# Products with the edge aggregates: one fp32 pass over 65 rows, or two fp32r passes over 128 rows

## The chip, the cores and the metric

The kernel runs on one core of one Trainium2 chip. The metric is the device time of one execution in microseconds (us), lower is better. The engines are TensorE (PE; its weight loads are PEld), VectorE (DVE), ScalarE (ACT), GpSimd (POOL) and SyncE (SP), which here only issues DMAs. Each engine runs its own list of instructions in order and waits on semaphores for the others.

## The reference

Two layers of a graph network over 1024 nodes of 512 features, each with a layer norm, a graph part, an attention-like mixer and a feed-forward part. The change is in the graph part of the second layer:

```python
def _L1_gnn_ref(x, edge_index, edge_attr, u, batch, W1, b1, W2, b2):
    col = edge_index[1]
    summed = jax.ops.segment_sum(edge_attr, col, num_segments=x.shape[0])      # 33792 edges, 64 features
    count = jax.ops.segment_sum(jnp.ones((edge_attr.shape[0],)), col, num_segments=x.shape[0])
    agg = summed / jnp.maximum(count, 1.0)[:, None]                            # 1024 x 64
    h = jnp.concatenate([x, agg], axis=-1)                                     # 1024 x 576
    h = jax.nn.relu(h @ W1 + b1)                                               # 1024 x 1024
    return x + h @ W2 + b2
...
x = x + _L0_ffn_ref(layernorm(x))          # 16 experts, each token goes to one
xn = layernorm(x)
x = x + _L1_gnn_ref(xn, ...) + _L1_mix_ref(xn, ...)
```

So `h @ W1 + b1` is a product with the 512 features of `xn`, one with the 64 aggregates, and a bias.

## The kernel before

Large products keep fp32 accuracy with fp32r operands: each operand is split in a high part (a copy rounded to fp32r, made by ACT) and a low part (the rest, made by DVE), and `mm3` (lines 877 to 881) issues low x high, high x high and high x low, three matmuls of 512 columns. `L879`, `L880` and `L881` are these three, in every stage. Engines meet at numbered jobs: `finished(eng, job)` waits until PE has completed the job, `emptied(eng, job)` until its PSUM bank has been read out.

The work around the change comes in this order.

- The 16 experts. For expert e, PE turns the rows (`eT`), and computes `eY`. ACT copies the expert's weights to the high part (`L1474`), DVE subtracts the low part (`L1978`), DVE adds the bias (`L2022`), and ACT sends the result to DRAM (`send_y`, `L1321`). SP loads the experts' weights (`L763`) into a ring of six, each load after `ew_split` says that both halves of an earlier expert are split; behind them it loads the graph weights W1a and W2a into `xn` (`L716`).
- After the last expert ACT and DVE split W1a and W2a (`split_weight`, `L1344` and `L1619`), while POOL gathers the experts' results by row (`L846`). PE transposes the aggregates (`aggT`, `L1124`), DVE copies them out of PSUM (`L2027`) and sets a row of ones for the bias (`L2028`).
- DVE then adds the gathered rows (`routed`, `L2033`), takes the moments (`L1632`, `L1633`), normalises (`L1646`) two rows of tiles at a time, and PE turns them (`turn_rows`, `L887`); ACT and DVE split what was turned (`L1350`, `L1626`). The tiles t = 0 to 3 come first, 4 to 7 after PE has begun.
- The products H: for hh (half of the 1024 hidden columns), th (half of the tokens) and m (block of 128 columns) twelve matmuls by `mm3` and one call of `from_aggregates` (`L1129`), which multiplies the 64 rows of aggregates and the row of ones with W1's last 64 rows and the bias. These operands are fp32, in `w1e` and `aggT` with 65 rows. For the four H of hh = 0, th = 0 this call comes first, ahead of the transposes, for the other twelve it comes last. The products HW (with W2) follow each group of four H.

The trace shows each `from_aggregates` as two matmul instructions.

Of the kernel before, what the change touches and what calls it, by code (L numbers as in the profile page):

```python
# [310 lines left out]
def build(nc, a):  # L311
# [18 lines left out]
    with ExitStack() as ctx:  # L330
# [3 lines left out]
        def f32(ap):  # L334
            return ap[:].bitcast(F32)
# [38 lines left out]

        aggT = arena[0:EA + 1, 2 * AW:2 * AW + N]
        w1e = arena[0:EA + 1, 2 * AW + N:2 * AW + 2 * N]
        pring = arena[:, 3 * AW:4 * AW].rearrange("p (r i) -> p r i", r=4)
# [150 lines left out]
        res_ready = sem("res_ready")  # L528
        w1e_in = sem("w1e_in")
        l1_in = sem("l1_in")  # L530
        rowa_in = sem("rowa_in")
# [146 lines left out]
        def _(sp):  # L678
# [107 lines left out]
            for e in range(WRING, EXPERTS):  # L786
                load_expert(e)
            sp.wait_ge(res_ready, T)
            load_weight("W1a")
            load_weight("W2a")  # L790
            finished(sp, "eY", EXPERTS - 1)
            sp.dma_start(w1e[0:EA], a["L1_gnn_W1"][D:D + EA]).then_inc(w1e_in, 16)
            sp.dma_start(w1e[EA:EA + 1], a["L1_gnn_b1"].rearrange("(a n) -> a n", a=1)).then_inc(w1e_in, 16)
            sp.wait_ge(res_ready, 2 * T)
# [72 lines left out]
        def _(pe):  # L867
# [253 lines left out]
            for g in range(2):  # L1121
                o = open_bank("aggT", g)
                for j in range(4):
                    ins = pe.transpose(o[0:EA, chunk(j)], agg[:, 4 * g + j, :], ident)  # L1124
                close(ins)

            def from_aggregates(hh, th, m, start):
                ch = hh * C + m
                return pe.matmul(at("H", hh, th, m), w1e[:, ch * P:(ch + 1) * P], aggT[:, th * HALF:(th + 1) * HALF],  # L1129
                                 start=start, stop=not start)  # L1130

            pe.wait_ge(w1e_in, 32)
            pe.wait_ge(blk_ready, 1)
            for g in range(2):
# [28 lines left out]

            pe.wait_ge(blk_ready, 2)
            o = open_bank("csq")
# [162 lines left out]
        def _(act):  # L1328
# [152 lines left out]
            for e in range(EXPERTS):  # L1481
                if e >= 2:
                    expert_high(e, 0)
                finished(act, "eT", e)
                act.activation(xbT[e % 2][:, 0], at("eT", e)[:, 0:C * CAPR].rearrange("p (c s) -> p c s", c=C), ACT.Copy).then_inc(xb_hi, 1)
                if e >= 2:
                    expert_high(e, 1)
                    send_y(act, e - 2)
            send_y(act, EXPERTS - 2)
            send_y(act, EXPERTS - 1)  # L1490
            split_weight("W1a")
            split_weight("W2a")
# [111 lines left out]
        def _(dve):  # L1604
# [404 lines left out]
            for e in range(EXPERTS + 1):  # L2009
# [6 lines left out]
                if e > 0:  # L2016
# [3 lines left out]
                    if y >= Y_RING:  # L2020
                        dve.wait_ge(y_out[y % Y_RING], 16 * (y // Y_RING))
                    dve.tensor_tensor(ey[y % Y_RING], at("eY", y)[0:CAPR, :], eb[y % 4], ALU.add).then_inc(evicted[bank_of[("eY", y)]], 1)  # L2022
            split_weight("W1a")
            split_weight("W2a")
            for g in range(2):
                finished(dve, "aggT", g)
                dve.tensor_copy(aggT[0:EA, g * HALF:(g + 1) * HALF], at("aggT", g)[0:EA, :]).then_inc(evicted[bank_of[("aggT", g)]], 1)  # L2027
            dve.memset(aggT[EA:EA + 1, :], 1.0).then_inc(blk_ready, 1)  # L2028
            dve.wait_ge(res_ready, T)
# [21 lines left out]
            for t in range(2, TH):  # L2051
                lo(("xT", 2, t))
            for t in range(TH, T):
                if t > TH:
                    routed(t)
                routed_moments(t)
# [261 lines left out]
```

## Time and profile before

| what | value |
|---|---|
| three runs | 906.35, 908.46, 911.83 us; median 908.46 us |
| the profiled execution | 909.68 us, span of its instructions 907.9 us |
| PE busy | 803.0 us, 88% of the span |
| PE weight loads | 575.9 us |
| DVE busy | 630.3 us, 69% |
| ACT busy | 372.4 us, 41% |
| POOL busy | 102.4 us, 11% |
| mean granted TensorE clock | 0.951 of full |

Busy times overlap between the engines. Matmuls are pipelined, and their ends are modelled: the distance from one start to the next tells what a matmul costs, not its own duration. "Idle before" is how long an engine had nothing to do, and the name behind it who released it.

### The profile page before, as it was taken

The page shows a single profiled execution, that of the slowest core. Times are in us where ns is not written, and L with a number is a line of the kernel's source. Part 1 is how long each engine was busy: PE and PEld are TensorE (multiplying, and loading weights), DVE is VectorE, ACT ScalarE, POOL GpSimd, SP SyncE. Part 2 cuts the span into 40 slices and gives each one's busy share as a digit, 9 for nine tenths or more (in the row PEclk, how much of TensorE's full clock was granted, in tenths as well). Part 3 has the DMA queues.
Part 4 walks back from the last instruction along what each step waited for, and adds up shares of the span by engine and source line. Part 5 has one row for each costly group of instructions (what it writes and reads, how often), then busy time and mean ns, then how long its engine had stood idle before and what let it go on. Part 6 is the DMA issues. An engine that isn't in the chain of part 4 may idle for free. (4 is left out here: it accounts for less than half of the span.)

```text
span 907.9 us, 11554 instructions
## 1 busy us (share of the span) xinstructions
PE 803.0 (88%) x4058; PEld 575.9 (63%) x4058; DVE 630.3 (69%) x1207; ACT 372.4 (41%) x557; POOL 102.4 (11%) x76
## 2 busy tenths in 40 slices
PE   5999999999999960895899998998797999999788
PEld 3777888888778840563587777555463445446564
DVE  7667776776749557598853232778867888884976
ACT  2342343332313240475112117756315887884150
POOL 3000000000000005012280004443100000000010
PEclk9989999999999995898599999999898999999999
DMA  5571312210302414996311102000001000000002
GB/s 173 150 250 49 107 56 71 71 36 8 117 1 92 147 65 138 286 373 233 97 66 47 47 22 72 1 1 1 2 2 48 1 1 1 1 0 1 6 1 93
DMA packets 48152, 66.63 MB, mean 73 GB/s; under 512 B 4268, under 2 KB 22460, under 8 KB 48095
## 3 DMA queue, kind: packets, MB, share of 16 engines
q1 hardware_dynamic: 43903, 56.22, 19.4%
q0 software_dynamic: 2384, 6.92, 2.3%
q10 hardware_dynamic: 1808, 2.75, 0.8%
q8 instruction: 33, 0.54, 0.2%
q14 instruction: 24, 0.20, 0.1%
HBM read 56.38 MB, written 9.50 MB: 73 GB/s over the span
## 5 line engine op out<-in xcount | busy, mean ns | idle before, releaser
L879 PE MATMUL bank<-xT,slot 128*128 128x512 f32 (+1 forms) x248 | 105.9, 427 | 5.7 <-DVE xT L1626 5.7
L880 PE MATMUL bank<-xT,slot 128*128 128x512 f32 (+1 forms) x248 | 98.5, 397 | 0.0
L881 PE MATMUL bank<-xT,slot 128*128 128x512 f32 (+1 forms) x248 | 98.2, 396 | 0.0
L1350 ACT ACTIVATE slot<-bank 128x512 fp32r<-128x512 f32 (+3 forms) x60 | 34.2, 586 | 144.3 <-PE bank L1129 56.3
L879 PE MATMUL bank<-slot 128*128 128x512 f32 (+1 forms) x212 | 85.2, 402 | 4.1 <-issue 1.8
L2131 DVE TENSOR_REDUCE key<-bank 128x2 f32<-128x1024 f32 x64 | 75.2, 1218 | 14.5 <-PE bank L1189 14.5
L879 PE MATMUL bank<-slot,xT 128*128 128x512 f32 (+1 forms) x192 | 79.2, 412 | 3.7 <-DVE arena L2194 2.8
L881 PE MATMUL bank<-slot 128*128 128x512 f32 (+1 forms) x212 | 81.9, 386 | 0.0
L880 PE MATMUL bank<-slot 128*128 128x512 f32 (+1 forms) x212 | 81.8, 386 | 0.0
L881 PE MATMUL bank<-slot,xT 128*128 128x512 f32 (+1 forms) x192 | 77.0, 401 | 0.0
L1563 ACT ACTIVATE arena<-bank 128x1024 f32<-128x1024 f32 x64 | 65.7, 1027 | 27.7 <-PE bank L1255 27.6
L880 PE MATMUL bank<-slot,xT 128*128 128x512 f32 (+1 forms) x192 | 77.0, 401 | 0.0
L879 PEld LDWEIGHTS bank<-xT,slot 128*128 128x128 f32 (+1 forms) x248 | 47.1, 190 | 21.5 <-issue 12.4
L880 PEld LDWEIGHTS bank<-xT,slot 128*128 128x128 f32 (+1 forms) x248 | 47.2, 190 | 11.0 <-issue 2.2
L881 PEld LDWEIGHTS bank<-xT,slot 128*128 128x128 f32 (+1 forms) x248 | 47.1, 190 | 11.2
L859 POOL TENSOR_TENSOR split_sq<-xn,split_sq 128x1024 fp32r<-128x1024 f32 x16 | 39.2, 2451 | 125.7 <-ACT split_sq L1526 125.7
L2174 DVE TENSOR_TENSOR slot<-arena,slot 128x1024 fp32r<-128x1024 f32 x43 | 52.4, 1218 | 0.2 <-ACT slot L1553 0.2
L879 PEld LDWEIGHTS bank<-slot 128*128 128x128 f32 x212 | 40.5, 191 | 15.7 <-issue 6.1
L833 POOL DMA_INDIRECT expert_rows<-xn,idx x8 | 10.2, 1276 | 322.3 <-DVE idx L1970 320.2
L879 PEld LDWEIGHTS bank<-slot,xT 128*128 128x128 f32 (+1 forms) x192 | 34.7, 181 | 18.1 <-issue 6.1
L881 PEld LDWEIGHTS bank<-slot 128*128 128x128 f32 x212 | 40.5, 191 | 8.2
L880 PEld LDWEIGHTS bank<-slot 128*128 128x128 f32 x212 | 40.6, 192 | 7.9 <-issue 0.7
(323 smaller groups left out, 1647.5 us busy)
## 6 DMA issues: line engine op xcount, KB each, us to landing
arena<-in_ewT SPq DMA_DIRECT2D x16, 1024.0 KB, 11.5
arena<-in_edge_attr SPq DMA_DIRECT2D x16, 512.0 KB, 4.0
wraw<-in_qkvT SPq DMA_DIRECT2D x3, 1024.0 KB, 5.2
expert_rows<-rows SPq DMA_DIRECT2D x1, 2560.0 KB, 14.0
wraw<-in_L_ffn_expert_b POOLq DMA_DIRECT2D x16, 160.0 KB, 5.8
expert_results<-wraw ACTq DMA_DIRECT2D x16, 160.0 KB, 5.7
xn<-in_x SPq DMA_DIRECT2D x4, 512.0 KB, 6.3
wraw<-in_L_mix_w_qkv SPq DMA_DIRECT2D x2, 1024.0 KB, 7.8
```

The costliest lines, as they stand in the source:

```text
L833: pool.indirect_dma_start(xbuf, bass.IndirectOffsetOnAxis(ap=idx[:, 0, t:t + 1], axis=0), xn[:, t, :], None).then_inc(rows_sent, 16)
L859: pool.tensor_tensor(split_sq[:, i % 4, 1], raw_sq[:, i % 4], f32(split_sq[:, i % 4, 0]), ALU.subtract).then_inc(sq_lo, 1)
L879: pe.matmul(out, L[1], R[0], start=start, stop=False, **kw)
L880: pe.matmul(out, L[0], R[0], start=False, stop=False, **kw)
L881: return pe.matmul(out, L[0], R[1], start=False, stop=stop, **kw)
L1350: act.activation(h, src, kw.pop("func", ACT.Copy), **kw).then_inc(hi_done, 1)
L1563: act.activation(pexp[:, n % 3], bank[:, b:b + 2, :], ACT.Exp).then_inc(evicted[b], 1)
L2131: dve.tensor_reduce(mxh[:, c % 2, jh, :, it:it + 1], bank[:, b:b + 2, :], AX, ALU.max).then_inc(evicted[b], 1)
L2174: dve.tensor_tensor(psplit(n % 3, 1), pexp[:, n % 3], f32(psplit(n % 3, 0)), ALU.subtract).then_inc(p_lo, 1)
```

## The change

`from_aggregates` issues two fp32r matmuls over 128 rows in place of one fp32 matmul over 65. The operands are stacked:

- `agg_rows[:, 0]` holds the high part of the aggregates in rows 0 to 63 and the low part in rows 64 to 127; `agg_w[:, 0]` holds the high part of the weights twice. Their product is high x high plus high x low.
- `agg_rows[:, 1]` holds the high part again in rows 0 to 63 and ones below; `agg_w[:, 1]` holds the low part of the weights, and below it zeros, with the bias' high part in row 64 and its low part in row 96.

To have the aggregates in all 128 rows, ACT writes `agg` twice side by side (`agg_twice`) behind its last work on expert 15, and PE transposes that. SP loads the 64 rows of W1 twice and the bias twice, after both halves of expert 11 are split (`ew_split` 24), ahead of W1a and W2a; before it loaded them once, after the last expert. ACT makes the high parts of these weights and of the bias (3 instructions) and of the transposed aggregates (4), ahead of splitting W1a. DVE fills (2 memsets), makes the low parts (2 and 2), splits W1a, and goes to the gathered rows; its part of splitting W2a moves behind the transposes' low parts of t = 0 to 3. The copies `L2027` and the memset `L2028` go.

```diff
--- before.py
+++ after.py
@@ -372,8 +372,11 @@
         ering = arena[:, AW:AW + WRING * C * D].rearrange("p (w c d) -> p w c d", w=WRING, c=C)
         gath = arena[:, AW:2 * AW].rearrange("p (t d) -> p t d", t=T)
 
-        aggT = arena[0:EA + 1, 2 * AW:2 * AW + N]
-        w1e = arena[0:EA + 1, 2 * AW + N:2 * AW + 2 * N]
+        agg_rows = nc.alloc_sbuf_tensor_at("agg_rows", [P, 2, N], F32R, offset=arena_at + 4 * 2 * AW)
+        agg_w = nc.alloc_sbuf_tensor_at("agg_weights", [P, 2, N], F32R, offset=arena_at + 4 * (2 * AW + 2 * N))
+        agg_twice = arena[:, 3 * AW:3 * AW + 2 * T * EA].rearrange("p (t v e) -> p t v e", t=T, v=2)
+        w1e = arena[:, 3 * AW + N:3 * AW + 2 * N]
+        b1e = arena[:, 3 * AW + 2 * N:3 * AW + 3 * N]
         pring = arena[:, 3 * AW:4 * AW].rearrange("p (r i) -> p r i", r=4)
         VW = T * HEADS * (HD + 1)
         vone = nc.alloc_sbuf_tensor_at("vone", [P, 2, T, HEADS, HD + 1], F32R, offset=arena_at + 4 * AW)
...
@@ -785,12 +793,14 @@
                 load_rows(group)
             for e in range(WRING, EXPERTS):
                 load_expert(e)
+            sp.wait_ge(ew_split, 2 * (EXPERTS - WRING + 2))
+            for v in range(2):
+                sp.dma_start(w1e[EA * v:EA * (v + 1)], a["L1_gnn_W1"][D:D + EA]).then_inc(w1e_in, 16)
+            for row in (EA, EA + 32):
+                sp.dma_start(b1e[row:row + 1], a["L1_gnn_b1"].rearrange("(a n) -> a n", a=1)).then_inc(w1e_in, 16)
             sp.wait_ge(res_ready, T)
             load_weight("W1a")
             load_weight("W2a")
-            finished(sp, "eY", EXPERTS - 1)
-            sp.dma_start(w1e[0:EA], a["L1_gnn_W1"][D:D + EA]).then_inc(w1e_in, 16)
-            sp.dma_start(w1e[EA:EA + 1], a["L1_gnn_b1"].rearrange("(a n) -> a n", a=1)).then_inc(w1e_in, 16)
             sp.wait_ge(res_ready, 2 * T)
             for name in ("W1b", "W2b", "Lq", "Lk", "Lv", "Lo"):
                 load_weight(name)
@@ -1120,17 +1130,20 @@
 
             for g in range(2):
                 o = open_bank("aggT", g)
+                pe.wait_ge(agg_copied, 2)
                 for j in range(4):
-                    ins = pe.transpose(o[0:EA, chunk(j)], agg[:, 4 * g + j, :], ident)
+                    ins = pe.transpose(o[:, chunk(j)], agg_twice[:, 4 * g + j].rearrange("p v e -> p (v e)"), ident)
                 close(ins)
 
             def from_aggregates(hh, th, m, start):
                 ch = hh * C + m
-                return pe.matmul(at("H", hh, th, m), w1e[:, ch * P:(ch + 1) * P], aggT[:, th * HALF:(th + 1) * HALF],
-                                 start=start, stop=not start)
-
-            pe.wait_ge(w1e_in, 32)
-            pe.wait_ge(blk_ready, 1)
+                o, w = at("H", hh, th, m), slice(th * HALF, (th + 1) * HALF)
+                pe.matmul(o, agg_w[:, 0, chunk(ch)], agg_rows[:, 0, w], start=start, stop=False)
+                return pe.matmul(o, agg_w[:, 1, chunk(ch)], agg_rows[:, 1, w], start=False, stop=not start)
+
+            pe.wait_ge(agg_high, 4)
+            pe.wait_ge(agg_w_high, 2)
+            pe.wait_ge(agg_ready, 1)
             for g in range(2):
                 emptied(pe, "aggT", g)
             for m in range(C):
@@ -1161,7 +1174,7 @@
                                 waits=lambda k: t == 0 and emptied(pe, "H", hh, th, k))
 
 
-            pe.wait_ge(blk_ready, 2)
+            pe.wait_ge(blk_ready, 1)
             o = open_bank("csq")
             for c in range(PAIRS):
                 ins = pe.matmul(o[:, c:c + 1], csquare[:, chunk(c)], ones[:, 0:1], start=True, stop=True)
@@ -1486,8 +1499,21 @@
                 if e >= 2:
                     expert_high(e, 1)
                     send_y(act, e - 2)
+            for v in range(2):
+                act.activation(agg_twice[:, :, v, :], agg[:, :, :], ACT.Copy).then_inc(agg_copied, 1)
             send_y(act, EXPERTS - 2)
             send_y(act, EXPERTS - 1)
+            act.wait_ge(w1e_in, 64)
+            act.activation(agg_w[:, 0, :], w1e, ACT.Copy).then_inc(agg_w_high, 1)
+            act.wait_ge(agg_filled, 1)
+            for row in (EA, EA + 32):
+                ins = act.activation(agg_w[row:row + 1, 1, :], b1e[row:row + 1], ACT.Copy)
+            ins.then_inc(agg_w_high, 1)
+            for g in range(2):
+                finished(act, "aggT", g)
+                w = slice(g * HALF, (g + 1) * HALF)
+                act.activation(agg_rows[:, 0, w], at("aggT", g), ACT.Copy).then_inc(agg_high, 1)
+                act.activation(agg_rows[0:EA, 1, w], at("aggT", g)[0:EA], ACT.Copy).then_inc(agg_high, 1)
             split_weight("W1a")
             split_weight("W2a")
             for g in range(2):
@@ -2020,12 +2046,18 @@
                     if y >= Y_RING:
                         dve.wait_ge(y_out[y % Y_RING], 16 * (y // Y_RING))
                     dve.tensor_tensor(ey[y % Y_RING], at("eY", y)[0:CAPR, :], eb[y % 4], ALU.add).then_inc(evicted[bank_of[("eY", y)]], 1)
+            dve.memset(f32(agg_w)[EA:P, 1, :], 0.0).then_inc(agg_filled, 1)
+            dve.memset(f32(agg_rows)[EA:P, 1, :], 1.0)
+            dve.wait_ge(agg_w_high, 2)
+            dve.tensor_tensor(agg_w[0:EA, 1, :], w1e[0:EA], f32(agg_w)[0:EA, 0, :], ALU.subtract)
+            low = slice(EA + 32, EA + 33)
+            dve.tensor_tensor(agg_w[low, 1, :], b1e[low], f32(agg_w)[low, 1, :], ALU.subtract).then_inc(agg_ready, 1)
+            for g in range(2):
+                dve.wait_ge(agg_high, 2 * g + 1)
+                w, lows = slice(g * HALF, (g + 1) * HALF), slice(EA, P)
+                dve.tensor_tensor(agg_rows[lows, 0, w], at("aggT", g)[lows], f32(agg_rows)[lows, 0, w], ALU.subtract).then_inc(
+                    evicted[bank_of[("aggT", g)]], 1)
             split_weight("W1a")
-            split_weight("W2a")
-            for g in range(2):
-                finished(dve, "aggT", g)
-                dve.tensor_copy(aggT[0:EA, g * HALF:(g + 1) * HALF], at("aggT", g)[0:EA, :]).then_inc(evicted[bank_of[("aggT", g)]], 1)
-            dve.memset(aggT[EA:EA + 1, :], 1.0).then_inc(blk_ready, 1)
             dve.wait_ge(res_ready, T)
             dve.wait_ge(rows_sent, 16 * T)
             def routed(t):
@@ -2050,6 +2082,7 @@
             routed(TH)
             for t in range(2, TH):
                 lo(("xT", 2, t))
+            split_weight("W2a")
             for t in range(TH, T):
                 if t > TH:
                     routed(t)
```

What stands in a row on PE around each of the twelve later calls, in the products H of hh = 0, th = 1 (`xT` is the turned xn, `slot` the weights, `arena` the aggregates and their weights). Before:

```order
L880 MATMUL bank<-xT,slot 128x512
L881 MATMUL bank<-xT,slot 128x512
L1129 MATMUL bank<-arena 128x512
L879 MATMUL bank<-xT,slot 128x512
L880 MATMUL bank<-xT,slot 128x512
```

And in the changed kernel, where mm3's lines are 889 to 891:

```order
L891 MATMUL bank<-xT,slot 128x512
L1141 MATMUL bank<-agg_rows,agg_weights 128x512
L1142 MATMUL bank<-agg_rows,agg_weights 128x512
L889 MATMUL bank<-xT,slot 128x512
L890 MATMUL bank<-xT,slot 128x512
```

One matmul became two, and nothing else moved there.

On DVE behind the last expert (`L2022` and `L2048` add its bias; `slot<-xn` is a weight's low part). Before:

```order
L2022 TENSOR_TENSOR wraw<-bank,wraw 80x512 x2
L1619 TENSOR_TENSOR slot<-xn,slot 128x2048 x2
L2027 COPY arena<-bank 64x512 x2
L2028 MEMSET arena 1x1024
L2033 SCALAR_TENSOR_TENSOR arena<-arena,cols 128x512 x2
L1632 BN_STATS cols<-arena 128x6
```

And now:

```order
L2048 TENSOR_TENSOR wraw<-bank,wraw 80x512 x2
L2049 MEMSET agg_weights 64x1024
L2050 MEMSET agg_rows 64x1024
L2052 TENSOR_TENSOR agg_weights<-arena,agg_weights 64x1024
L2054 TENSOR_TENSOR agg_weights<-arena,agg_weights 1x1024
L2058 TENSOR_TENSOR agg_rows<-bank,agg_rows 64x512 x2
L1645 TENSOR_TENSOR slot<-xn,slot 128x2048
L2065 SCALAR_TENSOR_TENSOR arena<-arena,cols 128x512 x2
L1658 BN_STATS cols<-arena 128x6
```

Six instructions stand where three stood, and one of the two weight splits is gone from here. It comes back further down, behind the low parts of the turned tiles (`xT<-bank,xT`). Before and now:

```order
L2033 SCALAR_TENSOR_TENSOR arena<-arena,cols 128x512
L1626 TENSOR_TENSOR xT<-bank,xT 128x4x128 x2
L1632 BN_STATS cols<-arena 128x6
```

```order
L2065 SCALAR_TENSOR_TENSOR arena<-arena,cols 128x512
L1652 TENSOR_TENSOR xT<-bank,xT 128x4x128 x2
L1645 TENSOR_TENSOR slot<-xn,slot 128x2048
L1658 BN_STATS cols<-arena 128x6
```

On ACT behind the last two results sent (`expert_results`), before and now:

```order
L1321 DMA expert_results<-wraw 80x512 [waits evicted7]
L1344 ACTIVATE slot<-xn 128x2048 [waits mm_done,w_in2]
L1344 ACTIVATE slot<-xn 128x2048 [waits mm_done,w_in3]
L1355 ACT_TABLE_LOAD
```

```order
L1334 DMA expert_results<-wraw 80x512 [waits evicted7]
L1507 ACTIVATE agg_weights<-arena 128x1024 [waits w1e_in]
L1510 ACTIVATE agg_weights<-arena 1x1024 [waits agg_rows_filled]
L1510 ACTIVATE agg_weights<-arena 1x1024
L1515 ACTIVATE agg_rows<-bank 128x512 [waits mm_done]
L1516 ACTIVATE agg_rows<-bank 64x512
L1515 ACTIVATE agg_rows<-bank 128x512 [waits mm_done]
L1516 ACTIVATE agg_rows<-bank 64x512
L1357 ACTIVATE slot<-xn 128x2048 [waits mm_done,w_in2]
L1357 ACTIVATE slot<-xn 128x2048 [waits mm_done,w_in3]
L1368 ACT_TABLE_LOAD
```

Seven instructions stand ahead of the high part of W1a, for which DVE waits.

## Rows read from the trace of the kernel before

**Rows 1.** Waits of PE from 445 to 560 us: engine, line, releaser, total, times, longest.

```profile
PE bank L879 <- DVE xT L1626: 1.5, 1, 1.5
```

**Rows 2.** Stretches: length, busy time by engine, granted clock (PEclk), DMA share, GB/s.

```profile
434.00:436.00 2.00, 2.00 (x4) 0.86 (x3) 1.93 (x6) 0.20 (x1) 1.70 (x2) 0.50 0.68 182
...
450.00:451.00 1.00, 1.00 (x5) 0.81 (x4) 0.97 (x2) 0.00 (x0) 0.00 (x0) 0.79 0.07 16
...
452.00:460.00 8.00, 8.00 (x42) 6.73 (x41) 4.20 (x9) 2.51 (x5) 5.66 (x5) 1.00 0.70 259
```

**Rows 3.** PE in order of time, 462 to 478 us: start, duration, instruction.

```profile
462.67 0.39 PE L879 MATMUL bank<-slot 128*128 128x512 f32 x1
...
471.29 0.39 PE L881 MATMUL bank<-slot 128*128 128x512 f32 x1
...
474.24 1.02 PE L1129 MATMUL bank<-arena 65*128 65x512 f32 x2
...
475.33 0.40 PE L880 MATMUL bank<-xT,slot 128*128 128x512 f32 x1
...
477.84 1.02 PE L1129 MATMUL bank<-arena 65*128 65x512 f32 x2
```

**Rows 4.** Line 1129 alone: durations, first and last start.

```profile
L1129 PE MATMUL bank<-arena x32: 590/592/1191, 431.2 to 536.1; 65*128 65x512 f32 x32
```

**Rows 5.** All engines in order of time, 422 to 446 us.

```profile
422.25 3.71 ACT L1344 ACTIVATE slot<-xn 128x2048 fp32r<-128x2048 f32 x2 [5.26 <-PE bank L1124]
424.19 4.49 DVE L1619 TENSOR_TENSOR slot<-xn,slot 128x2048 fp32r<-128x2048 f32 x2 [2.39 <-ACT slot L1344]
...
430.14 0.91 DVE L2028 MEMSET arena<- 1x1024 f32 x1 [0.27 <-issue]
431.09 1.59 DVE L2033 SCALAR_TENSOR_TENSOR arena<-arena,cols 128x512 f32<-128x512 f32 x2
...
431.16 7.16 PE L1129 MATMUL bank<-arena 65*128 65x512 f32 x8 [9.20 <-DVE arena L2028]
...
436.08 1.00 DVE L1646 TENSOR_SCALAR xn<-arena,cols 128x512 f32<-128x512 f32 x2
...
438.12 1.91 PE L887 MATMUL bank<-kst,xn 128*128 128x128 f32 x8
...
440.56 0.20 ACT L1355 ACTIVATE cols<-cols 128x2 f32<-128x2 f32 x1
...
441.49 1.00 DVE L1646 TENSOR_SCALAR xn<-arena,cols 128x512 f32<-128x512 f32 x2
...
443.25 0.60 ACT L1350 ACTIVATE xT<-bank 128x512 fp32r<-128x512 f32 x1 [2.49 <-PE bank L887]
...
445.57 0.76 PE L879 MATMUL bank<-xT,slot 128*128 128x512 f32 x1 [1.50 <-DVE xT L1626]
```

**Rows 6.** Groups by line and shape, ACT and DVE, 395 to 425 us.

```profile
L1474 ACT ACTIVATE slot<-arena 128x1024 fp32r<-128x1024 f32 x14 | 14.8, 1055 | 6.5 <-PE bank L881 6.5
L1978 DVE TENSOR_TENSOR slot<-arena,slot 128x1024 fp32r<-128x1024 f32 x15 | 18.1, 1207 | 0.0
```

**Rows 7.** In order of time, 452 to 460 us: tiles 4 to 7, and four ACT copies.

```profile
452.12 1.91 DVE L1646 TENSOR_SCALAR xn<-arena,cols 128x512 f32<-128x512 f32 x4
...
458.86 1.91 PE L887 MATMUL bank<-kst,xn 128*128 128x128 f32 x16
...
459.55 2.07 ACT L1350 ACTIVATE xT<-bank 128x512 fp32r<-128x512 f32 x4
```

**Rows 8.** SP's DMA issues, 395 to 401 us.

```profile
396.35 3.63 SPq L763 DMA_DIRECT2D arena<-in_ewT  x2
400.03 3.25 SPq L716 DMA_DIRECT2D xn<-in_L_gnn_W  x1
```

**Rows 9.** DMA issues from 395 us on: size, median us from issue to landing.

```profile
arena<-in_ewT SPq DMA_DIRECT2D x2, 1024.0 KB, 14.5
xn<-in_L_gnn_W SPq DMA_DIRECT2D x2, 1024.0 KB, 17.7
```

More of the change, by code:

```diff
@@ L529, in build @@
         w1e_in = sem("w1e_in")
+        agg_copied = sem("agg_copied")
+        agg_high = sem("agg_rows_high")
+        agg_w_high = sem("agg_weights_high")
+        agg_ready = sem("agg_rows_ready")
+        agg_filled = sem("agg_rows_filled")
         l1_in = sem("l1_in")
```

## The prediction

> **What bounds the kernel now.** I read the waits first, then the order of time around line 1129. From 445 to 560 us, where all products H and HW lie, PE waits once, 1.5 us at the very start [rows 1]: that stretch is bound by PE, and an instruction that PE loses there shortens it by its full slot. Ahead of it, from 422 to 445 us, the order of time shows the opposite: PE idles 9.20 us until DVE's memset, runs eight pieces of line 1129, then turns tiles as DVE delivers them [rows 5]. There the chain is ACT's high part of W1a, DVE's low parts, copies and memset, the gathered rows, the normalised tiles, their transposes. So the change is priced twice: slots of PE behind 445.6 us, lateness of DVE's chain before.
>
> **PE's slots.** The durations of pipelined matmuls overlap, so I count starts. From 462.67 to 471.29 us there are 38 steps of one 128x512 product: 8.62 / 38 = 0.227 us each [rows 3]. One block H goes from 474.24 to 477.84 us, 3.60 us; its twelve products take 12 x 0.227 = 2.72, which leaves 0.88 us for the call of line 1129 [rows 3]. The 32 pieces are 16 calls [rows 4], 12 of them at the end of a block, in the PE-bound stretch. Two fp32r products cost 2 x 0.227 = 0.45 us, if operands in 128 rows stream as all other operands do. Saved: 0.88 - 0.45 = 0.43 us a call, 12 x 0.43 = 5.2 us. The matmuls behind them read nothing new, and what waits for H (ACT's and DVE's reads) only comes sooner.
>
> The four early calls take 7.16 us, at a granted clock of 0.50 [rows 2, 5], the 1.2 GHz level. As eight products at that level they take 8 x 2 x 0.21 = 3.4 us. They count only as far as they hold up the first transposes: tile 0 is normalised half of 1.00 us behind 436.08, at 436.6, while PE comes free and starts turning at 438.12 [rows 5]. Those 1.5 us are what the early calls cost now.
>
> **The chain on ACT and DVE ahead of the gathered rows.** ACT is free for this at 422.25 [rows 5]. Three copies of 1024 columns: 1.06 us each, overlapping to some 0.96 [rows 6], so 2.9 us. (No row has a copy on one partition. I take the 128-partition price, the dearest; the 0.20 us of a two-column ACTIVATE [rows 5] bounds it below, 1.5 us less for both.) Four copies out of PSUM: 2.07 us for four tiles [rows 7]. The high part of W1a follows at 422.25 + 2.9 + 2.0 = 427.2 and takes 1.9 (half of 3.71, rows 5), until 429.0. DVE's two memsets (0.91 each by the 1x1024 one, which lie in its idle time of 2.39 us, rows 5) and four subtractions (2 x 1.21 [rows 6], 2 x 0.7) fit between: weights from 425.2 to 427.6, aggregates to 429.05. Then W1a's low part, 2.25 (half of 4.49), until 431.3. The gathered rows start at 431.3 where they started at 431.09 [rows 5]: 0.2 us later. Gone are W2a's low part, both copies and the memset; the ACT work put ahead of W1a takes nearly all of that back. PE's early products run from 429.1 to 432.5, out of everybody's way.
>
> Then the rest of the chain moves by 0.2: tile 0 is ready at 436.85 instead of 436.6, but PE is free, so it is turned at once. DVE's low parts of tiles 0 and 1, which waited for ACT, follow its moments without the gap, and the normalisation of tiles 2 and 3, at 441.49 now, comes at about 440.85. From it to PE's first product of H the distance stays 445.57 - 441.49 = 4.1 us [rows 5]. H starts at 444.9: **0.65 us gained**. Bounds: if the copies on one partition are as short as they may be, 1.5 more at most, less what DVE then lacks (its own subtractions end at 429.05 less the same), together 2.1; if no copy overlaps the next and each handover costs 0.2 us, 1.4 less, -0.7.
>
> **What is moved.** W2a's low part, 2.25 us, now stands ahead of the moments of tiles 4 to 7. Their normalisation starts at 452.12 now and PE turns them at 458.86 [rows 7], 6.7 us later. In the change it starts at 452.1 + 2.25 - 0.65 = 453.7, and PE comes at 458.2: covered, with 4.5 us to spare; without that cover each us costs one. POOL's additions and the loads of W1b and W2b wait for the same tiles, and move by 1.6 us; POOL needs its first result only where HW is read, behind 461 us.
>
> **DMA.** SP issues expert 15's load at 399.6 and W1a's at 400.03 [rows 8]; they land 14.5 and 17.7 us later, one behind the other [rows 9]. Now SP waits for two experts more, 2 x 3.26 = 6.5 us (the distance of two loads in rows 8: 3.63 - 0.37), until 406.1, and issues 0.5 MB in four DMAs before W1a. Expert 15's load lands near 414, so the queues never run dry; the stacked weights land by 416, W1a by 419.5 and W2a by 422.3. ACT wants them at 422.25, 427.2 and 429: hidden. The aggregates' two copies stand on ACT while PE still has experts 14 and 15: hidden.
>
> **Sum.** 5.2 + 0.65 = 5.85 us off the profiled execution's 909.68 gives 903.8. The runs before have the median 908.46, which gives 902.6; I predict between, **903.3 us**. By its unknowns this case goes from 901 to 906.
>
> **The granted clock.** H begins at 445.57 at the low level, which still holds in 434 to 436; from 450 to 451 it is 0.79, and 1.00 after [rows 2]: the clock comes up at about 450.4. So 4.8 us of H run at half speed, which costs 2.4 us. The early calls, 7.16 us of unbroken PE work, did not lift it [rows 2, 5]. The Trainium skill ("TensorE: Matmul & The Clock Gate", "What's actually happening") has it that the throttled state is the default and sustained activity releases it. Here it did not for the fp32 products. By the page's rule nothing sets the fp32r ones apart, by the trace fp32r products did lift it at 450.4.
>
> **Rivals.**
> - *The clock comes up for H sooner*, since the early calls are now of the kind that lifts it. Gain up to 2.4 us more: 901.0. Against it: between 432.5 and 436.9 PE is idle, longer than now, and transposes alone did not lift it either.
> - *It comes up later*, or drops once more, by as much: 905.7. For it: less PE work ahead of H; against it: the stretch from 445 on is as dense as before.
> - *ACT's chain is the new wait.* Seven copies with no overlap take 3 x 1.06 + 4 x 0.60 = 5.6 for 4.9, with handovers 6.3. Each us shifts W1a's low part, the gathered rows and H by one. The gain is 5.2 - 0.7 = 4.5: 904.6.
> - *The fp32r pair brings nothing*: if the pair still took 0.88, the start alone stays, 908.4. Against it stand all steps of 0.227 in rows 3; operands of lines 879 to 881 have the same form.
> - *SP's queue turns the sign.* W1a's issue occupies SP for 3.25 us with full queues [rows 8]. If each of the four new DMAs does so too, W1a is issued at 406.1 + 13 = 419.1 and, landing 17.7 us later, is there at 436.8 for 427.2. DVE's chain is late by 9.6, less the 5.85: 3.8 us slower, 912.8. It decides from 427.2 + 5.85 = 433 on. Against it: two of the four carry 4 KB, and by then nothing but expert 15's load is queued.
>
> **How the numbers follow.** Forecast 0.55; clock sooner 0.09, later 0.09; ACT's chain 0.14; no saving 0.07; SP's queue 0.06. Single runs before lie 906.35 to 911.83 apart, so a median moves by 1.5 or so without any cause. From 900.0 to 907.0 us the range leaves out the last two cases, half of the clock's early one at its far end, and little of the rest. A measurement tells 0.5% from nothing, 4.5 us. The forecast's 5.85 lies 1.3 above that, so it counts 0.75 as faster; the sooner clock fully; of the later clock and ACT's chain four in ten. Faster 0.60, within 0.5% 0.34, slower 0.06.
>
> **What would show it.** Twelve blocks H of 3.18 us where they were 3.60; the early products over by about 432.5; the gathered rows from 431.3; the first transposes right behind the first normalised tile; H at 444.9; PE without a wait at tiles 4 to 7; W1a landed before 427. I am wrong if a block stays at 3.6, if the gathered rows begin later than 433, or if PE waits for tile 4.

## The result and the profile after

The changed kernel took 902.64 us, the median of 20 runs (898.71 to 907.72), against 907.07 for the kernel before on the same chips (20 runs, 905.13 to 911.83). The ratio over all of these runs is 0.9944, 95% interval 0.9929 to 0.9960: 5.1 us faster, between 3.6 and 6.4. (The two medians alone lie 4.4 us apart.) The forecast was 903.3 us, a gain of 5.85 us. The profiled execution took 903.49 us, its span 901.7. Of the executions behind this document, one of the run `both` (947.57 us) and two of the kernel before that were taken beside it (1301.79 and 1928.99 us) were in a slower state, and the ratios and the medians given leave them out.

The first part of the profile's page, busy time by engine (before: 803.0, 630.3 and 372.4 us for PE, DVE and ACT):

```profile
PE 795.4 (88%) x4058; PEld 576.2 (64%) x4058; DVE 634.7 (70%) x1210; ACT 378.3 (42%) x566; POOL 103.0 (11%) x76
```

PE has as many instructions as before (a call was two pieces and is two products) and is busy 7.6 us less; DVE and ACT are busy 4 and 6 us more. What shortened is PE's list, and the chain through the other two had to bear more work. In order of time on PE, one block H of the changed kernel, against [rows 3]:

```profile
471.25 0.39 PE L1141 MATMUL bank<-agg_rows,agg_weights 128*128 128x512 f32 x1
471.48 0.39 PE L1142 MATMUL bank<-agg_rows,agg_weights 128*128 128x512 f32 x1
471.71 0.39 PE L889 MATMUL bank<-xT,slot 128*128 128x512 f32 x1
...
474.43 0.39 PE L1141 MATMUL bank<-agg_rows,agg_weights 128*128 128x512 f32 x1
```

The two products start 0.23 us apart like any others, and the block takes 3.18 us where it took 3.60. The same stretch as in [rows 5], all engines in order of time, from the last expert's bias add on:

```profile
418.67 0.69 DVE L2048 TENSOR_TENSOR wraw<-bank,wraw 80x512 f32<-80x512 f32 x1 [1.34 <-PE bank L891]
...
419.74 1.06 ACT L1507 ACTIVATE agg_weights<-arena 128x1024 fp32r<-128x1024 f32 x1 [3.50 <-DVE wraw L2048]
...
420.82 2.12 ACT L1510 ACTIVATE agg_weights<-arena 1x1024 fp32r<-1x1024 f32 x2
...
422.97 1.22 DVE L2052 TENSOR_TENSOR agg_weights<-arena,agg_weights 64x1024 fp32r<-64x1024 f32 x1 [1.36 <-ACT agg_weights L1510]
...
425.02 3.71 ACT L1357 ACTIVATE slot<-xn 128x2048 fp32r<-128x2048 f32 x2
...
426.96 2.29 DVE L1645 TENSOR_TENSOR slot<-xn,slot 128x2048 fp32r<-128x2048 f32 x1 [0.21 <-ACT slot L1357]
427.00 0.76 PE L1141 MATMUL bank<-agg_rows,agg_weights 128*128 128x512 f32 x1 [7.50 <-DVE agg_rows L2058]
...
429.18 1.41 DVE L2065 SCALAR_TENSOR_TENSOR arena<-arena,cols 128x512 f32<-128x512 f32 x2
...
434.58 1.97 PE L897 MATMUL bank<-kst,xn 128*128 128x128 f32 x8 [3.82 <-DVE xn L1672]
...
442.44 0.76 PE L889 MATMUL bank<-xT,slot 128*128 128x512 f32 x1 [1.50 <-DVE xT L1652]
```

The bias add ends at 419.36 here. In the kernel before it ended at 421.81:

```profile
421.12 0.69 DVE L2022 TENSOR_TENSOR wraw<-bank,wraw 80x512 f32<-80x512 f32 x1 [1.33 <-PE bank L881]
```

These 2.45 us can't be laid to the change: in eight profiles of kernels that are the same up to there (the change's among them), the add ended anywhere between 418.5 and 424.0 us. So distances are what to compare. PE's early products are over 3.8 us before the first transposes, which now follow the first normalised tile. Up to W1a's low part ACT sets the pace: DVE waits 1.36 us for the copies of the bias and 0.21 for W1a's high part. From there on it is DVE's.

The executions, cut at three events: the end of DVE's bias add of expert 15, the start of PE's first product of H, and the start of the second product behind the last call of the aggregates. (It is the second because the first one's row, 0.80 us long, begins inside the call where the call is fp32.) The last cut, before and after:

```profile
536.76 0.40 PE L880 MATMUL bank<-slot 128*128 128x512 f32 x1
```

```profile
528.60 0.39 PE L890 MATMUL bank<-slot 128*128 128x512 f32 x1
```

In us:

| stretch | before | after | difference |
|---|---|---|---|
| start to the last expert's bias add | 421.81 | 419.36 | -2.45 |
| from there to the first product of H | 23.76 | 23.08 | -0.68 |
| from there to the second product behind the last call | 91.19 | 86.16 | -5.03 |
| the rest of the span | 371.14 | 373.10 | +1.96 |

The two stretches of the change, in the middle, give -5.71 us. The first holds only the loads moved ahead and ACT's two copies of `agg`, the last holds no edit, and both differ by no more than profiles of kernels do that are the same there. The last one differs by the clock; these are its stretches, first of before, then of after, to be read at PEclk (third number from the end):

```profile
536.00:908.00 372.00, 333.48 (x1442) 204.90 (x1440) 273.04 (x376) 203.44 (x281) 44.51 (x20) 0.97 0.05 16
```

```profile
528.00:902.00 374.00, 335.97 (x1443) 207.07 (x1441) 273.01 (x376) 203.41 (x281) 44.51 (x20) 0.96 0.05 15
```

DVE, ACT and POOL do the same work to 0.03 us, and only PE's busy time follows the granted clock. In thirteen profiles of kernels that are the same from there on, the last stretch took 368.7 to 373.4 us. A forecast of 5 us is therefore read from the distances, and the medians of many runs only confirm it.

### The profile page after: what moved, and what is told of

It is laid out like the page before. It is cut to its first block and busy times, and to the rows that moved or that the text cites. A ratio compares the mean times of both kernels' runs of the same rounds, so it can differ in the third digit from the quotient of the medians.

```text
span 901.7 us, 11571 instructions
## 1 busy us (share of the span) xinstructions
PE 795.4 (88%) x4058; PEld 576.2 (64%) x4058; DVE 634.7 (70%) x1210; ACT 378.3 (42%) x566; POOL 103.0 (11%) x76
## 5 line engine op out<-in xcount | busy, mean ns | idle before, releaser
L889 PE MATMUL bank<-slot 128*128 128x512 f32 (+1 forms) x212 | 83.3, 393 | 4.0 <-issue 1.8
L891 PE MATMUL bank<-slot 128*128 128x512 f32 (+1 forms) x212 | 81.6, 385 | 0.0
L890 PE MATMUL bank<-slot 128*128 128x512 f32 (+1 forms) x212 | 81.5, 384 | 0.0
```

What stands on the lines that cost most here:

```text
L889: pe.matmul(out, L[1], R[0], start=start, stop=False, **kw)
L890: pe.matmul(out, L[0], R[0], start=False, stop=False, **kw)
L891: return pe.matmul(out, L[0], R[1], start=False, stop=stop, **kw)
```

## Experiments

All times of the runs are medians, and each ratio is to the kernel before as timed beside that run; "distance" is that from the last bias add's end to H's first product (23.76 before, 23.08 after), from one profile of each.

| run | median us (runs) | ratio to before, interval | rows after add | distance |
|---|---|---|---|---|
| the change | 902.64 (20) | 0.9944, 0.9929 to 0.9960 | 9.82 | 23.08 |
| late_fp32 | 908.39 (12) | 1.0010, 0.9994 to 1.0027 | 9.82 | 23.10 |
| early_fp32 | 904.11 (10) | 0.9958, 0.9938 to 0.9977 | 9.82 | 23.09 |
| w2a_back | 901.98 (6) | 0.9940, 0.9919 to 0.9960 | 12.02 | 25.30 |
| late_load | 904.19 (12) | 0.9967, 0.9952 to 0.9982 | 13.71 | 26.98 |
| before_w2a_later | 905.40 (12) | 0.9982, 0.9967 to 0.9997 | 8.02 | 21.86 |
| clock_kept | 897.27 (6) | 0.9895, 0.9876 to 0.9914 | 9.82 | 22.39 |
| weights_early | 900.96 (7) | 0.9946, 0.9918 to 0.9974 | 8.13 | 22.67 |
| both | 899.05 (5) | 0.9906, 0.9881 to 0.9932 | 8.13 | 21.92 |

"Rows after add" is the start of DVE's first gathered row behind that add (9.28 before).

### The twelve later calls as one fp32 matmul

```diff
+                if not start:
+                    return pe.matmul(o, f32(agg_w)[:, 0, chunk(ch)], f32(agg_rows)[:, 0, w], start=False, stop=True)
```

> The changed kernel, with the twelve later calls as one fp32 matmul over the same 128 rows (the second product, with the weights' low part and the bias, is left out there; the four early calls stay two fp32r products). My theory: the gain lies in these slots. A block H takes 3.60 us again (12 x 0.227 + 0.88) where it takes 3.17 now, the twelve cost 12 x 0.43 = 5.2 us, and the time is about 907.8 against 902.6; the distance from the last expert's bias add to the first product of H stays 23.1 us. Rival: the gain came from the chain ahead of H and from a slower start of the kernel before; then the time stays within 1.5 us of 902.6.

Measured: 908.39 us, 5.75 above the change, all of the gain gone, with the distance unmoved. PE in order of time:

```profile
474.45 1.02 PE L1142 MATMUL bank<-agg_rows,agg_weights 128*128 128x512 f32 x2
474.91 0.80 PE L889 MATMUL bank<-xT,slot 128*128 128x512 f32 x1
...
478.08 1.02 PE L1142 MATMUL bank<-agg_rows,agg_weights 128*128 128x512 f32 x2
```

A block takes 3.63 us, 0.45 more than with two fp32r products, and with 128 rows nearly what it took with 65 (3.60). Twelve times 0.45 is 5.4. The stretch from H's start to the second product behind the last call took 90.45 us in this profile, 4.3 more than in the change and not 5.4: the clock came up 2.9 us behind H's start here and 5.3 there, and 2.4 us less at half speed are worth 1.2. The theory of the slots stands, the rival falls.

### The four early calls as one fp32 matmul

```diff
+                if start:
+                    return pe.matmul(o, f32(agg_w)[:, 0, chunk(ch)], f32(agg_rows)[:, 0, w], start=True, stop=False)
```

> The changed kernel, with the four early calls as one fp32 matmul each over 128 rows (the second product is left out in those four; the twelve later calls are as changed). They take 7.2 us again in place of 3.4, but lie ahead of the first transposes, which come 7.5 us behind their start. Theory: the fp32r form lifted the clock (the changed kernel has it at 1.00 from about 431 to 434 us, the kernel before stayed at 0.50 through 7.16 us of fp32 products). Then this run stays at 0.50 from 427 to the middle of H, and its time is within 1 us of the changed kernel's, since the lifted clock fell again before H. Rival: the form has nothing to do with it and only the place in time decides; then the clock rises during the early fp32 products too.

Measured: the distance, 23.09, is the change's, as expected of work off the path. The time, 904.11, is 1.5 us above the change's, where under 1 was expected, but the two intervals overlap widely. The theory of the clock was wrong. Three stretches of 2 us, PEclk third from the end:

```profile
428.00:430.00 2.00, 2.00 (x3) 0.74 (x3) 2.00 (x3) 1.75 (x2) 1.83 (x1) 0.50 0.52 137
430.00:432.00 2.00, 2.00 (x5) 0.61 (x3) 1.90 (x5) 0.00 (x0) 1.56 (x2) 0.91 0.57 143
432.00:434.00 2.00, 0.21 (x1) 0.00 (x0) 1.93 (x6) 0.20 (x1) 1.47 (x2) 1.00 0.74 172
```

The clock rose during fp32 products too, at about 430.4 us, and the rest of them ran fast. The form is not the cause; the last three experiments come back to it.

### DVE's low part of W2a back in its old place

```diff
             split_weight("W1a")
+            split_weight("W2a")
...
                 lo(("xT", 2, t))
-            split_weight("W2a")
```

> The changed kernel, with DVE's low part of W2a back in its old place, right behind that of W1a and ahead of the gathered rows. Theory: DVE is the chain there, so the gathered rows and the first product of H come 2.3 us later (25.4 us behind the last expert's bias add in place of 23.1), and the time is 904.9. Rival: the gathers' landing holds the rows up, so that 2.3 us of DVE work ahead of them cost under 1 us: 902.6 to 903.5.

DVE and PE in order of time:

```profile
435.30 1.41 DVE L2066 SCALAR_TENSOR_TENSOR arena<-arena,cols 128x512 f32<-128x512 f32 x2
...
448.58 0.77 PE L889 MATMUL bank<-xT,slot 128*128 128x512 f32 x1 [1.50 <-DVE xT L1652]
```

The add ends at 423.28 here: the rows start 12.02 us behind it, 2.20 later than in the change, and H 25.30, 2.22 later. In the chain the theory holds to 0.1 us. The median does not show it: 901.98 of six runs, where 904.9 was expected. Its interval, 0.9919 to 0.9960, leaves out 0.9968, which is the change's ratio and the 2.2 us, by less than the change's own interval is wide. The rest of the span was 369.2 us in this profile against 373.1 in the change, and 369.0 in clock_kept, where H is early; whether a later H helps it or the six runs fell well is open.

### The weights' last rows loaded behind the experts

```diff
-            sp.wait_ge(ew_split, 2 * (EXPERTS - WRING + 2))
-            for v in range(2):
-                sp.dma_start(w1e[EA * v:EA * (v + 1)], a["L1_gnn_W1"][D:D + EA]).then_inc(w1e_in, 16)
-            for row in (EA, EA + 32):
-                sp.dma_start(b1e[row:row + 1], a["L1_gnn_b1"].rearrange("(a n) -> a n", a=1)).then_inc(w1e_in, 16)
             sp.wait_ge(res_ready, T)
             load_weight("W1a")
             load_weight("W2a")
+            finished(sp, "eY", EXPERTS - 1)
+            for v in range(2):
+                sp.dma_start(w1e[EA * v:EA * (v + 1)], a["L1_gnn_W1"][D:D + EA]).then_inc(w1e_in, 16)
+            for row in (EA, EA + 32):
+                sp.dma_start(b1e[row:row + 1], a["L1_gnn_b1"].rearrange("(a n) -> a n", a=1)).then_inc(w1e_in, 16)
```

> The changed kernel, with the four DMAs of W1's last rows and the bias issued behind the last expert, as the kernel before does with its two. Theory: ACT's first copy waits for them: four issues of 0.5 us and a landing of 2 to 3 us put it at about 4.5 us behind PE's last product of the experts instead of 1.1, so the gathered rows and H come 3 to 3.5 us later, and the time is 905.6 to 906.1. Rival: the load is hidden in both places, as it was in the kernel before; then the time stays at 902.6 and the early load brings nothing.

```profile
422.25 1.06 ACT L1507 ACTIVATE agg_weights<-arena 128x1024 fp32r<-128x1024 f32 x1 [8.03 <-DMA arena<-in_L_gnn_b]
```

The add ends at 417.97; ACT begins 4.28 us behind it, released by the bias' DMA, where it began 0.38 behind it in the change. The distance grew by 3.90 us, where 3 to 3.5 were expected, all of that wait. The median grew by 1.55, to 904.19 where 905.6 to 906.1 was expected, and 0.9967 stands against the change's 0.9944 with intervals that overlap: in the chain the theory holds, and the time alone shows neither it nor its rival. The early load is needed by this form of the products: the kernel before needed its operands 9.3 us behind the add and could load late.

### The kernel before, with W2a's low part later

The same move as the change's, in the kernel before: `split_weight("W2a")` taken from behind that of W1a and put behind `lo(("xT", 2, t))` of tiles 2 and 3.

> The kernel before (one fp32 matmul a call), with the one change that DVE's low part of W2a stands behind the low parts of tiles 2 and 3, where the change put it. Theory: the move is what shortens the chain, and the change spends nearly all of it on ACT's seven copies. Then here the gathered rows start 7.0 to 7.8 us behind the last expert's bias add in place of 9.28, PE's early fp32 calls (7.16 us) then hold up the first transposes by about 1 us, and H starts 21.8 to 22.2 us behind that add in place of 23.76: 1.8 us off the kernel before, about 0.998 of its time. Blocks H stay at 3.60 us. Rival: the chain gains nothing from the move (the gathers' landing is what the rows wait for); then the distance stays at 23.8.

```profile
429.55 0.75 DVE L2032 SCALAR_TENSOR_TENSOR arena<-arena,cols 128x512 f32<-128x512 f32 x1 [0.97 <-DMA arena<-expert_results,idx]
430.91 0.75 DVE L2032 SCALAR_TENSOR_TENSOR arena<-arena,cols 128x512 f32<-128x512 f32 x1 [0.61 <-DMA arena<-expert_results,idx]
...
443.39 0.76 PE L879 MATMUL bank<-xT,slot 128*128 128x512 f32 x1 [1.50 <-DVE xT L1626]
```

The move alone shortens the distance by 1.90 us, to 21.86, and the kernel by 0.18% (0.03 to 0.33). That is more than the 0.68 us of the whole change. By this difference, the change's seven ACT copies and six DVE instructions spend 1.2 us of what the move brings. DVE now waits for the gathers' landing, 0.97 and 0.61 us: the chain has reached its next limit, and the rows start 8.02 us behind the add where 7.0 to 7.8 was expected. PE's early calls held the transposes up by nothing that shows: these start 0.60 us behind the normalisation, as in the change, where 1 us more was expected.

### Products nobody reads, ahead of H

```diff
+FILL = (11, 8, 6)
...
-            for t in range(TH):
+            def keep_busy(bank_at, count):
+                for _ in range(count):
+                    pe.matmul(bank[:, bank_at, :], agg_w[:, 0, chunk(0)], agg_rows[:, 0, 0:HALF], start=True, stop=True)
+
+            open_bank("xT", 2, 3)
+            keep_busy(bank_of[("xT", 2, 3)], FILL[0])
+            for t in range(2):
+                turn_rows(2, t)
+            keep_busy(bank_of[("xT", 2, 3)], FILL[1])
+            for t in range(2, TH):
                 turn_rows(2, t)
+            emptied(pe, "xT", 2, 0)
+            keep_busy(bank_of[("xT", 2, 0)], FILL[2])
```

> The changed kernel, with products nobody reads in PE's idle time ahead of H: 11 behind the early calls, 8 behind the transposes of tiles 0 and 1, 6 behind those of tiles 2 and 3, each 128x512 fp32r into a bank that is written over later or has been read. Theory: H starts at the low clock level because PE idles ahead of it, and that costs 2.4 to 2.6 us. Then the granted clock is 1.00 at H's start, the stretch from H's start to its last call takes 83.1 us in place of 85.7, the transposes are shorter by 0.5 us twice, and the time is 899.5 to 900. Rival: the filling products hold the transposes up by as much as the clock gives back (they run at half speed until the clock rises); then the time stays within 1 us of 902.6. A second rival: the clock falls in spite of them, and H takes 85.7 us.

PE in order of time, and the stretch at H's start:

```profile
429.57 2.68 PE L1155 MATMUL bank<-agg_rows,agg_weights 128*128 128x512 f32 x11
433.69 1.11 PE L898 MATMUL bank<-kst,xn 128*128 128x128 f32 x8 [1.44 <-DVE xn L1684]
434.56 2.09 PE L1155 MATMUL bank<-agg_rows,agg_weights 128*128 128x512 f32 x8
438.09 1.12 PE L898 MATMUL bank<-kst,xn 128*128 128x128 f32 x8 [1.44 <-DVE xn L1684]
438.96 1.62 PE L1155 MATMUL bank<-agg_rows,agg_weights 128*128 128x512 f32 x6
440.85 0.47 PE L890 MATMUL bank<-xT,slot 128*128 128x512 f32 x1 [0.27 <-DVE xT L1664]
```

```profile
440.00:442.00 2.00, 1.73 (x8) 1.17 (x7) 2.00 (x3) 0.00 (x0) 0.00 (x0) 1.00 0.04 8
```

The transposes find the clock at 1.00 and take 1.11 instead of 1.97 us. The distance fell by 0.69 us, and from H's start to its last call it took 83.29 us instead of 85.71, 2.42 less, which is the forecast's 2.4. That is 3.1 us by the distances. The median fell by 5.4, to 897.27 (by the ratios, 4.4), below the 899.5 to 900 expected; in the profile the rest of the span was 4.1 us shorter too, which these products do not touch, so more than 3.1 is not shown to be theirs. Both rivals fall. It has the lowest median here, and its interval and the change's do not overlap.

### The weights' work out of the chain, and both together

```diff
+            pool.wait_ge(ew_split, 2 * EXPERTS)
+            pool.memset(f32(agg_w)[EA:P, 1, :], 0.0).then_inc(agg_filled, 1)
+            pool.memset(f32(agg_rows)[EA:P, 1, :], 1.0).then_inc(agg_filled, 1)
...
             send_y(act, EXPERTS - 2)
+            act.wait_ge(w1e_in, 64)
+            act.wait_ge(ew_split, 2 * EXPERTS)
+            act.activation(agg_w[:, 0, :], w1e, ACT.Copy).then_inc(agg_w_high, 1)
             send_y(act, EXPERTS - 1)
...
+            split_weight("W1a")
```

The last line stands twice, on ACT and on DVE, each time ahead of the aggregates' parts.

> The changed kernel, with the work for the aggregates' weights taken out of the chain: GpSimd does both memsets as soon as expert 15's weights are split, ACT makes the weights' high part ahead of sending the last expert's result, and W1a's split stands ahead of the transposed aggregates' four copies on ACT and their low parts on DVE. Theory: DVE's gathered rows start 8.0 us behind the last expert's bias add in place of 9.82, the gathers' landing takes back up to 0.9 us of it, and H starts 21.5 to 22.1 us behind the add in place of 23.1: the time is 901.0 to 901.6. Rival: the gathers' landing is the next wait in full (the first is issued 3.9 us behind the add and lands 3.6 later, the others follow 1.3 to 2 us apart), and under 0.5 us is left: 902.1 and more.

```profile
427.79 0.75 DVE L2069 SCALAR_TENSOR_TENSOR arena<-arena,cols 128x512 f32<-128x512 f32 x1
...
429.71 0.75 DVE L2069 SCALAR_TENSOR_TENSOR arena<-arena,cols 128x512 f32<-128x512 f32 x1 [1.17 <-DMA arena<-expert_results,idx]
```

The first row starts 8.13 us behind the add, 1.69 earlier; the second then waits 1.17 us for its gather, and of the 1.69 only 0.41 reaches H (22.67). The rival was right in the chain: under 0.5 us is left. The median, 900.96, is what the theory expected and not the rival's 902.1, but its interval does not tell it apart from the change's.

> The two versions before this one together: the weights' work out of the chain, and products nobody reads in PE's idle time. If the two gains are independent, H starts 21 us behind the last expert's bias add and takes 83.1 us to its last call: 898 to 898.6. If the filling products now stand in the way of the transposes, which come sooner, the time is that of the better one of the two alone.

Measured: distance 21.92 and 83.29 us to the last call, 105.21 in sum against 105.68 in clock_kept and 108.79 in the change. In the distances the two gains add up (0.41 and 0.69 on their own, 1.16 together); H does not start at the 21 us expected because weights_early brings only 0.41. The median is 899.05, above the 898 to 898.6 expected and above clock_kept's 897.27, and its interval overlaps clock_kept's: the half microsecond is not to be seen in the time.

### What made the clock rise

The early calls stand above as fp32r over 128 rows (the change) and as fp32 over 128 rows (early_fp32). The three kernels here, each with one profile, have them as fp32 over 65 rows, as fp32r over 65, and as fp32r over 128 in the same place and number as the second.

> The changed kernel, with the four early calls as one fp32 matmul each over 65 of the 128 rows (the rest of their product is left out). It differs from early_fp32 in the rows alone. Seen so far: the clock came up at 430 to 433 us during or right behind early calls over 128 rows, of fp32 (early_fp32) and of fp32r, and stayed at 0.50 through 7.16 us of fp32 over 65 rows (the kernel before, and before_w2a_later). Theory: the count of rows is what matters; then the clock stays at 0.50 from the early calls to the middle of H. Rival: the place in time decides; then it rises at 430 to 434 here as well. The time is told by a single run and decides nothing: 899 to 907.

> The changed kernel, with each of the four early calls as four fp32r products over 65 of the rows in place of two over 128 (what they compute is not the reference's part; two of the four are repeats): 16 x 0.43 = 6.8 us of unbroken work at the low level. Theory of the rows: the clock stays at 0.50 through them, as under fp32 over 65 rows. Rival, the form: fp32r lifts it, so it rises to 1.00 within them.

> The same sixteen early fp32r products over all 128 rows (repeats, not the reference's part): the counterpart of early_fp32r_65. Both theories: the clock rises within them, so that the rest of them runs at 0.23 us each and the sixteen take under 6.8 us. If it does not rise here, rows and form are both out, and the place in time decides.

Line of the early calls in each, fp32 over 65 rows, then fp32r over 65, then fp32r over 128:

```profile
L1142 PE MATMUL bank<-agg_rows,agg_weights x8: 1061/1061/1192, 428.2 to 434.3; 65*128 65x512 f32 x8
```

```profile
L1143 PE MATMUL bank<-agg_rows,agg_weights x16: 628/628/766, 426.8 to 433.4; 65*128 65x512 f32 x16
```

```profile
L1143 PE MATMUL bank<-agg_rows,agg_weights x16: 387/628/763, 431.7 to 437.3; 128*128 128x512 f32 x16
```

And a stretch of 2 us near the end of these products in the second, and in the third:

```profile
432.00:434.00 2.00, 2.00 (x5) 1.00 (x4) 1.92 (x6) 0.20 (x1) 1.57 (x2) 0.50 0.74 174
```

```profile
436.00:438.00 2.00, 1.71 (x7) 1.02 (x5) 1.90 (x6) 0.20 (x1) 1.39 (x3) 0.94 0.66 215
```

Over 65 rows the clock stayed at 0.50 through 7.2 us of unbroken products, in fp32 and in fp32r, and came up only after H had begun; over 128 rows it rose within them, in both forms. The theory of the rows stands on these two pairs of profiles, one in each form, and on the kernel before and before_w2a_later (65 rows, 7.2 us, no rise). It does not say all: late_fp32 is the change itself up to H, its early products took the same 3.75 us, and the clock did not rise there before H. The times of these three, 901.97, 903.81 and 905.75 us, are of single runs and tell nothing.

## Why the prediction was right

- **PE's slots** (forecast 5.2 us less). 5.03 measured from H's start to behind its last call, block by block 3.60 to 3.18. Confirmed by late_fp32, which gives it all back. The missing 0.2 is the clock: it came up 5.3 us behind H's start instead of 4.8, at about 447.7.
- **The chain** (forecast 0.65 us less). 0.68 measured. The mechanism was right: ACT's copies eat what the moved split gives, and before_w2a_later shows both sides, 1.90 less by the move and, by difference, 1.22 spent. That the number is so near is luck: two errors of a third of a us cancel. The gathered rows start 0.54 us later against the add, not 0.2. Most of this is ACT's three copies of weights and bias, forecast at 2.9 us with an overlap, which took 3.2 (419.74 to 422.96), one behind the other. Behind the rows the chain gave back 1.22 us (13.26 from the first row to H where it was 14.48), not 0.85.
- **What was moved.** PE turned tiles 4 to 7 without a wait (from 444 to 560 us it waits twice, 2.8 us in all, for ACT, behind 553 us and not for these tiles), W2a's low part ran beside H.
- **DMA.** SP issued the four new DMAs in 2.0 us and the loads of W1a and W2a behind them at once:

```profile
403.36 1.17 SPq L798 DMA_DIRECT2D arena<-in_L_gnn_W  x2
404.57 0.73 SPq L800 DMA_DIRECT2D arena<-in_L_gnn_b  x2
405.35 0.94 SPq L724 DMA_DIRECT2D xn<-in_L_gnn_W  x2
```

The two issues take 0.94 us together, where W1a's alone took 3.25 [rows 8]. They now come 8.5 us behind the last expert's load and not right behind it; that this distance is the reason is likely, and no run shows it alone. The rival of SP's queue falls with it. The two loads landed 14.9 us behind their issue (median), so W1a at about 420.3, and it was wanted at 425.0.

- **The clock.** The rival "sooner" had the mechanism and not the effect: the clock rose to 1.00 at about 430.6 us, as the early products ended, and it was back at 0.50 just behind 434, with PE idle from 430.8 to 434.6. PEclk is third from the end:

```profile
430.00:432.00 2.00, 0.76 (x2) 0.03 (x1) 1.93 (x4) 0.03 (x1) 1.39 (x3) 0.84 0.45 129
...
434.00:436.00 2.00, 1.42 (x7) 1.43 (x8) 1.93 (x5) 0.27 (x1) 1.05 (x2) 0.51 0.65 211
```

  H began at the low level, as forecast. When the clock then comes up is not the kernel's alone: in the eleven profiles without products that nobody reads it came 2.9 to 6.2 us behind H's start, which is worth up to 1.7 us of time; that 5.3 us lies so near the forecast's 4.8 is luck too. The prediction sets the trace against the rule drawn from the Trainium skill, because 7.16 us of products did not lift the clock, and reads the form, fp32 against fp32r, as the reason. That such work did not lift it stands, in four profiles, and the measurement decides. The form is not the reason: the clock rose during fp32 products over 128 rows in early_fp32, and not during fp32r products over 65.

The runs' range, 898.71 to 907.72, is wider than the effect; the forecast's median, 903.3 for 902.64, is as near as that allows.

## What to carry to other kernels

Price a matmul by the distance of starts, not by its duration or by what it computes: at the full clock one fp32 product costs 0.88 us over 65 rows and 0.91 over 128, and two fp32r products over 128 rows 0.45, so rows left empty can take the other half of a split operand for nothing on PE. Look for the work that the new form needs beside the matmul, and ask which engine paces the stretch it lands in: here seven ACT and six DVE instructions stood in a chain, in place of three, and cost 1.2 us that only the moved split paid for. And where a gap of PE lies ahead of a dense stretch, the clock level at which that stretch begins may be worth as much as the change.

## What the runs showed of the hardware that I had not expected

- Products over 65 rows did not lift TensorE's granted clock from its lower level (0.50, 1.2 GHz) in 7.2 us of unbroken work, in four profiles, fp32 and fp32r. Products over 128 rows, with PE no busier, were followed by the rise 3.2 to 4.9 us behind their start in seven profiles, in both forms. In two more, late_fp32 and w2a_back, 3.75 us of 128-row products were followed by none before H, though the change's 3.75 us of the same products were: what decides between these is not shown, and no row count but 65 and 128 was tried.
- 25 products whose result nobody reads, 6.4 us of work in the 7.7 us that PE idles between the early products and H, held the clock at 1.00 and gave 3.1 us by the distances.
- An ACT copy of 1024 columns on one partition takes 1.06 us, as on 128 (two in 2.12 us).
- A stretch of 370 us that no edit touches differs by 4 us between profiles, the change's and clock_kept's, with the granted clock alone: 0.96 against 0.98, 335.97 against 332.03 us of PE's busy time.
